# Logits of the last two batches from eight more output columns, and the placement of the last rows ahead of the border

## What is computed

```
x = x + attention(layernorm(x), ctx, ctx)    # 16 heads of 16; row i sees j < i (row 0 sees itself)
                                             # W_q, W_k, W_v, b_v, W_o, b_o
xt = layernorm(x) as 2048 rows
logits = xt @ wg                             # 8 experts
topv, topi = top_k(softmax(logits), 2); topv = topv / sum(topv)
pos = place of a row in its expert's queue: all first choices in row order, then all second choices
valid = pos < 512; gate = topv * valid; disp[topi, pos] += xt row where valid
h = relu(disp @ w1 + b1)                     # 256 -> 1024, for each expert
y = h @ w2 + b2                              # 1024 -> 256
out = x + sum over both choices of gate * y[topi, pos]
```

## Time and profile before

| | |
|---|---|
| median of three runs | 420.03 us (419.73 to 420.23) |
| the profiled execution | 422.05 us, of which the span is 420.3 |
| mean granted TensorE clock | 0.939 of full speed |
| busy: TensorE, its weight loads | 368.3 (88%), 315.2 (75%) |
| busy: VectorE, ScalarE, POOL | 294.4 (70%), 188.5 (45%), 214.6 (51%) |

### The profile page before, as it was taken

One profiled execution on the slowest core, in us unless ns is written; L12 is line 12 of the kernel. 1 busy time (PEld: TensorE's weight loads), 2 busy tenths in 40 slices (PEclk: granted clock), 3 DMA queues, 4 the chain that ended last, 5 costly groups with the idle time before them and its releaser, 6 DMA issues. The chain is left out here.

```text
span 420.3 us, 8189 instructions
## 1 busy us (share of the span) xinstructions
PE 368.3 (88%) x3030; PEld 315.2 (75%) x3030; DVE 294.4 (70%) x627; ACT 188.5 (45%) x258; POOL 214.6 (51%) x305
## 2 busy tenths in 40 slices
PE   3788889999999999777417999999999999999991
PEld 3656677878797877555305998989999999989891
DVE  6676778788887777837733777676778777776840
ACT  5423557565656557660203536263524435262410
POOL 8659866767677545250447008163463617060632
PEclk9988999999999999995556999999999999999998
DMA  7873815261706082413218009164363809040323
GB/s 219 236 215 121 212 31 153 76 193 39 201 14 191 18 218 83 153 51 114 52 38 292 22 2 264 51 218 97 134 176 75 240 18 272 27 58 2 37 27 37
DMA packets 38315, 49.15 MB, mean 117 GB/s; under 512 B 7138, under 2 KB 34180, under 8 KB 37252
## 3 DMA queue, kind: packets, MB, share of 16 engines
q1 hardware_dynamic: 29636, 34.93, 28.0%
q0 software_dynamic: 6144, 8.33, 10.5%
q10 hardware_dynamic: 2496, 5.38, 4.0%
HBM read 27.60 MB, written 8.41 MB: 86 GB/s over the span
## 5 line engine op out<-in xcount | busy, mean ns | idle before, releaser
L1578 POOL DMA_INDIRECT out_dram<-Y,scatter_idx x32 | 51.3, 1603 | 104.8 <-DVE Y L1734 89.4
L1621 ACT ACTIVATE hr<-ps,b_sb 128x512 f32<-128x512 f32 x64 | 43.2, 687 | 99.1 <-PE ps L1778 63.2
L764 DVE TENSOR_REDUCE nm<-ps 128x2 f32<-128x512 f32 (+1 forms) x96 | 62.5, 682 | 16.7 <-PE ps L1064 15.9
L1788 PE MATMUL ps<-w_hi,h_hi 128*128 128x256 f32 x224 | 63.2, 282 | 0.0
L1788 PE MATMUL ps<-w_lo,h_hi 128*128 128x256 f32 x224 | 62.5, 279 | 0.0
L1788 PE MATMUL ps<-w_hi,h_lo 128*128 128x256 f32 x224 | 62.5, 279 | 0.0
L529 ACT ACTIVATE PT<-ps 128x1536 f32<-128x1536 f32 x32 | 46.5, 1453 | 22.3 <-PE ps L1080 21.7
L1709 DVE CAST h_hi<-hr 128x512 fp32r<-128x512 f32 x60 | 27.5, 459 | 39.0 <-ACT hr L1621 38.9
L1778 PE MATMUL ps<-XT_hi,w_hi 128*128 128x512 f32 x128 | 51.5, 402 | 1.5 <-DVE XT_lo L1692 1.5
L1778 PE MATMUL ps<-XT_lo,w_hi 128*128 128x512 f32 x128 | 51.1, 399 | 0.0
L1778 PE MATMUL ps<-XT_hi,w_lo 128*128 128x512 f32 x128 | 51.1, 399 | 0.0
(11 more groups left out here) (234 smaller groups left out, 893.1 us busy)
## 6 DMA issues: line engine op xcount, KB each, us to landing
raw<-in_L_ffn_w_dram SPq DMA_DIRECT2D x12, 1024.0 KB, 8.2
raw<-in_L_ffn_w_dram ACTq DMA_DIRECT2D x4, 1024.0 KB, 5.5
c_sb<-in_ctx_dram SPq DMA_DIRECT2D x8, 256.0 KB, 3.8
xn_rows<-x2n SPq DMA_DIRECT2D x8, 256.0 KB, 3.0
out_dram<-x_all SPq DMA_DIRECT2D x8, 256.0 KB, 2.9
x_all<-in_x_dram SPq DMA_DIRECT2D x1, 1280.0 KB, 6.4
w_lo<-k_h SPq DMA_DIRECT2D x9, 128.0 KB, 2.5
w_hi<-q_h SPq DMA_DIRECT2D x9, 128.0 KB, 2.5
```

What stands on the lines that cost most here:

```text
L764: dve.tensor_reduce(nm[:, tile, h:h + count], max_bank[u % 2].rearrange("p (h j) -> p h j", h=count), AX_X, ALU.max, negate=True).then_inc ...
L1578: pool.indirect_dma_start(out_rows[:, :], bass.IndirectOffsetOnAxis(ap=scatter_idx[:, ST * e + j:ST * e + j + 1], axis=0), Y[q][:, j, :], ...
L1621: act.activation(hr[c % 2][:, :], h_bank[c % 4], ACT.Relu, bias=b1_sb[q][:, c:c + 1]).then_inc(hr_ready, 1)
L1788: last = pe.matmul(y_bank[j // 2][:, (j % 2) * D:(j % 2 + 1) * D], a[c % 4][:, j * P:(j + 1) * P], w[q][:, c, :], start=(c == 0 and n == 0 ...
```

## The change

1. **Logits without the turned x2n, for batches 6 and 7.** The layernorm's rows are (x - mean) times a factor, and the logit's order doesn't depend on the factor. x is the residual with its bias plus attention times W_o. So the kernel centres the router by its mean over the 256 inputs (wg_mid), puts W_o times wg_mid beside W_o as eight more columns (wo_hi and wo_lo have 264 columns), and gets eight logit columns from the same products that make the output rows (folded_outputs). The part from x with the bias is computed ahead: turn_biased, copy_biased, pre_router and copy_pre in step 7. sum_logits adds the two. The factor goes into the exponential (folded_ratio). turn_x2, copy_x2 and router fall away for these two batches; they stay for batches 0 to 5.
2. **What prepares this**, ahead of step 0: four transposes of W_o, the router's mean, and W_o times wg_mid, on TensorE between the score units of step -1, with copies on ScalarE and three small steps on VectorE.
3. **Early placement.** Its one-hot, counts, positions and numbers move from step 8 to step 7. The in_slot comparisons become 28 tensor_scalar of 128 elements with a scalar for each partition, where they were four tensor_tensor of 896; spart is f32 for this.
4. **Late placement, ahead of the border.** One-hot, counts, eq, in_slot (four tensor_scalar), late gates, table and gather_idx stand at the end of step 8. SP stores the late gates and then the last batch's output, and waits for all of it before the border. Behind the border POOL begins with the gathers.
5. **Weights of the first expert.** Parts 2 and 3 move from step 7 to step 8 on ScalarE, and behind the border on VectorE.
6. In step 7 POOL's mask of the last head group stands ahead of the powers of the layernorm, and on TensorE the transposes of x2n and the router give their places at the end of step 7 to early_counts and pre_router.

The core of the diff:

```diff
-    spart = sb("spart", [P, TOPK, EARLY], BF16)
+    spart = sb("spart", [P, TOPK, EARLY], F32)
...
+                if s == B:
+                    sp.wait_ge(gates_ready, 2)
+                    sp.dma_start(gate_tiles[:, 0:EARLY, :], gates[:, 0:EARLY, :]).then_inc(gates_stored, 16)
+                    for t in range(2):
+                        sp.wait_ge(x2n_ready, 2 * (s - 1) + t + 1)
+                        sp.dma_start(xn_tiles[s - 1][:, t, 0:D], x2n[:, t, :]).then_inc(x2n_stored, 16)
+                    sp.wait_ge(late_gates_ready, 2)
+                    sp.dma_start(gate_tiles[:, EARLY:, :], gates[:, EARLY:, :]).then_inc(gates_stored, 16)
+                    sp.dma_start(out_tiles[s - 1], x_all[:, 2 * (s - 1):2 * s, :]).then_inc(x2_stored, 16)
...
-            sp.wait_ge(gates_ready, 2)
-            sp.dma_start(gate_tiles[:, 0:EARLY, :], gates[:, 0:EARLY, :]).then_inc(gates_stored, 16)
-            sp.wait_ge(gates_stored, 16)
+            sp.wait_ge(gates_stored, 32)
             sp.wait_ge(spare_row, 32)
-            sp.wait_ge(x2n_stored, 16 * (B + 1))
+            sp.wait_ge(x2n_stored, 16 * (B + 2))
             sp.wait_ge(x2_stored, 16 * B)
...
                     mask(s, 2)
-                if out_part(s):
-                    powers(s - 1, ln2_stats, mv2, ve2, rs2, ln2_pow)
+                    mask(s, 3)
                 if s == B:
                     early_tiles(0)
                     early_tiles(1)
+                    last_powers(0)
+                    last_powers(1)
+                    late_gate()
+                    late_tiles()
+                elif out_part(s):
+                    powers(s - 1, ln2_stats, mv2, ve2, rs2, ln2_pow)
...
-                    first_weights(2, 3)
+                    copy_biased(0)
+                    copy_biased(1)
                     exp(s, 0)
                     round_attention(s)
                     exp(s, 1)
-                    first_weights(3, 4)
+                    copy_pre(0)
                     exp(s, 2)
                     values(s, 0)
                     exp(s, 3)
+                    copy_pre(1)
+                    values(s, 1)
                     normalise_x2(s)
-                    copy_x2(s)
-                    values(s, 1)
+                    early_ratio()
                     prefetch(3)
+                elif s == B:
+                    round_attention(s)
+                    early_rows()
+                    first_weights(2, 4)
+                    normalise_last(0)
+                    late_ratio()
+                    normalise_last(1)
+                    late_rows()
...
+            def sum_logits(s, t):
+                if t == 0:
+                    dve.wait_ge(pre_ready, folded(s) + 1)
+                dve.wait_ge(last_out, 2 * folded(s) + t + 1)
+                last = dve.tensor_tensor(lg[:, t, :], bank[t][:, D:D + EXPERTS], pre[:, folded(s), t], ALU.add)
+                if t == 1:
+                    last.then_inc(lg_ready, 1)
...
+            def last_rows():
+                n = B - 1
+                sum_logits(B, 1)
+                dve.wait_ge(lg_ready, n + 1)
+                for t in range(2):
+                    dve.max(top8[:, t, :], lg[:, t, :]).then_inc(top_ready, 1)
+                add_row_tile(B, 1)
+                dve.wait_ge(top_ready, 4 * n + 2)
+                for t in range(2):
+                    dve.max_index(idx8[:, t, :], top8[:, t, :], lg[:, t, :]).then_inc(top_ready, 1)
+                row_stats(B, 1)
+                dve.wait_ge(top_ready, 4 * n + 4)
+                for k in range(TOPK):
+                    dve.tensor_copy(expert_all[:, k, bass.ds(2 * n, 2)], idx8[:, :, k]).then_inc(top_used, 1)
+                dve.tensor_tensor(dl_all[:, bass.ds(2 * n, 2)], top8[:, :, 1], top8[:, :, 0], ALU.subtract).then_inc(top_used, 1)
+                row_moments(B, 1)
+                dve.wait_ge(top_used, 3 * n + 2)
+                late_onehots()
...
+            def late_places():
...
+                for k in range(TOPK):
+                    for t in range(2):
+                        last = dve.tensor_scalar(in_slot[:, k, EARLY + t, :], iota_s[:, :], late_spart[:, k, t:t + 1], None, ALU.is_equal)
+                last.then_inc(late_in_slot_ready, 1)
...
             def early_slots(k, n):
-                cols = slice(n * EARLY // 2, (n + 1) * EARLY // 2)
-                dve.tensor_tensor(in_slot[:, k, cols, :], spart[:, k, cols].unsqueeze(2).broadcast_to([P, EARLY // 2, P]),
-                                  iota_s[:, :].unsqueeze(1).broadcast_to([P, EARLY // 2, P]), ALU.is_equal).then_inc(in_slot_ready, 1)
+                for t in range(n * EARLY // 2, (n + 1) * EARLY // 2):
+                    last = dve.tensor_scalar(in_slot[:, k, t, :], iota_s[:, :], spart[:, k, t:t + 1], None, ALU.is_equal)
+                last.then_inc(in_slot_ready, 1)
...
-                    first_weights(2)
-                    add_output(s)
-                    dve.wait_ge(mask_done, 2 * GROUPS * (s + 1))
-                    first_weights(3)
-                    logits(s)
+                    add_rows(s, 0)
+                    sum_logits(s, 0)
+                    sum_logits(s, 1)
+                    top_two(s - 1)
+                    early_onehot()
+                    add_rows(s, 1)
+                    early_positions()
+                    early_numbers()
                 elif s == B:
-                    early_onehot()
                     normalise(s, 0)
                     normalise(s, 1)
-                    early_positions()
+                    early_groups()
+                    early_slots(0, 0)
                     split_attention(s)
-                    early_numbers()
-                    add_last(0)
-                    add_last(1)
-                    early_gates()
-                    early_groups()
-                    dve.wait_ge(ln2_pow, 4 * B)
-                    early_slots(0, 0)
                     early_slots(0, 1)
                     early_slots(1, 0)
                     early_slots(1, 1)
-                    logits(s)
+                    early_gates()
+                    add_rows(s, 0)
+                    sum_logits(s, 0)
+                    last_rows()
+                    late_places()
+                    late_gate()
+                    gather_rows()
...
+            def turn_output_weights():
+                pe.wait_ge(wqkvo_loaded[3], 16)
+                pe.wait_ge(k_rest_ready, 1)
+                pe.wait_ge(const_ready, 1)
+                turn(first_bank[1], lambda t: w_raw[:, 3, t, :], wo_turned)
...
+            def logit_weights():
+                pe.wait_ge(wg_mid_ready, 1)
+                pe.wait_ge(wo_copied, 1)
+                for f in range(2):
+                    for k in range(2):
+                        last = pe.matmul(first_bank[2][:, (2 + f) * EXPERTS:(3 + f) * EXPERTS], x2T[:, k, f * P:(f + 1) * P], wg_mid[:, k, :],
+                                         start=(k == 0), stop=(k == 1))
+                last.then_inc(wog_done, 1)
...
+            def pre_router(n):
+                pe.wait_ge(xb_copied, n + 1)
+                if n == 1:
+                    pe.wait_ge(pre_ready, 1)
+                for t in range(2):
+                    for k in range(2):
+                        last = pe.matmul(ps[:, 1, (2 * n + t) * EXPERTS:(2 * n + t + 1) * EXPERTS], xbT[n][:, k, t * P:(t + 1) * P],
+                                         wg_mid[:, k, :], start=(k == 0), stop=(k == 1))
+                last.then_inc(pre_done, 1)
...
+            def folded_outputs(s):
+                pe.wait_ge(aT_lo_ready, s)
+                pe.wait_ge(norm_done, 2 * s)
+                for t in range(2):
+                    m = 0
+                    for k in range(2):
+                        for a, w in ((aT_hi, wo_hi), (aT_lo, wo_hi), (aT_hi, wo_lo)):
+                            m += 1
+                            last = pe.matmul(fold_out(t), a[:, k, t * P:(t + 1) * P], w[:, k, :], start=(m == 1), stop=(m == 6))
...
-                    early_counts()
                     turn_last(lambda t: attn[:, t].rearrange("p h d -> p (h d)"), norm_done, at_done)
-                    last_outputs()
-                    turn_last(lambda t: x2n[:, t, :], x2n_ready, x2t_done)
+                    folded_outputs(s)
+                    late_counts()
                     early_table(0, 0)
-                    router(s)
                     early_table(0, 1)
                     early_table(1, 0)
                     early_table(1, 1)
+                    late_table()
...
+                    turn_biased(0)
+                    turn_biased(1)
                     turn_values(s, 0)
                     turn_values(s, 1)
                     b_scores(s, 0)
+                    pre_router(0)
                     turn_attention(s)
                     b_scores(s, 1)
                     values(s, 0)
                     b_scores(s, 2)
-                    outputs(s)
```

(18 more changed lines are left out.)

291 lines of the change are left out of this document (197 added, 94 removed).

## The result

The changed kernel takes 415.55 us (median of 14 runs, 414.24 to 420.76), the kernel before 420.62 (median of 14 runs, 419.71 to 428.36). The ratio is 0.9863, with a 95% interval of 0.9823 to 0.9902: 4 to 7 us less. Disturbed runs are left out of all ratios here. The forecast was 414.7 with a range of 411.2 to 418.6, faster. The profiled execution has a span of 414.4 us, against 420.3.

What follows compares the result with a forecast made beforehand. TensorE alone bounds from 224.38 us; VectorE's work ahead sets when the first gather starts. That gather 5.85 us sooner, less 0.5 ahead of attention, gives 5.3: 420.03 - 5.3 = 414.7 us, range 411.2 to 418.6.

Steps and rivals of the forecast that it cites:

- End of step 7: TensorE's first turn of step 8 starts at about 187.85 us, where it was 189.62.
- The clock: First turn of step 8 runs at 2.4 GHz, half of 1.95 us; normalisations end at 189.7, before 193.39.
- Comparisons and POOL: VectorE, eq to last sums: 28 comparisons 3.9 us, POOL's products 1.9, attention split 0.7, early gates 0.5.
- The dear rival: VectorE's small comparisons start 0.26 us apart: 28 cost 3.4 us more, the late four 0.5; 418.6 us; chance 0.14.
- the slower one: VectorE's small comparisons don't overlap, 0.35 us each: 32 cost 6.7 us more, 421.4 us; chance 0.07.
- The last logits: End of step 8, VectorE: 1.1 + 1.3 + 1.0 + 0.4 us bring the one-hot to 201.6, where it was 210.16.
- Late placement: End of step 8: one-hot to in_slot's end 2.8 us, gates ready at 205.0, VectorE done at 206.75.
- The border: Ahead of the gathers: the last output lands at 208.1, 1.35 us later than VectorE; border's 0.54 makes it 208.65.
- From the gather to layer 1: First gather to first layer-1 matmul: 8.95 us, carried over as unchanged.
- Ahead of attention: Added TensorE and VectorE work between the first score units costs 0.5 us, bounds 0 and 2.6.
- less in the way: Comparisons slip past POOL's products (-1.9), output lands before VectorE is done (-1.35), or both: 412.8, 413.3, 411.4; chance 0.22.
- The low clock at 188: TensorE at step 8's start is granted 1.2 GHz all the same, +0.9 us; chance 0.06, shared with the prologue case.

Runs made afterwards that it cites:

- e_chain: Changed kernel with the last batch's logits waiting again for the normalised, turned and routed x2n (results unused), both tiles' sums ahead; 423.74 us, 1.0046 of the kernel before.
- e_store: Changed kernel with the last batch's output stored as soon as its sums are there, ahead of x2n and the late gates; 415.27 us, 0.9863 of the kernel before.
- e_split: Changed kernel with the second half of the first expert's weight split on VectorE behind the turned rows; 416.57 us, 0.9892 of the kernel before.
- e_gate: Changed kernel with the output stored early and VectorE's late gates ahead of the late eq; 414.44 us, 0.9774 of the kernel before.
- e_best: e_order plus TensorE matmuls of no use, six in step 7 and 26 between border and layer 1; 411.0 us, 0.9733 of the kernel before.
- e_order: Changed kernel with large early comparisons, POOL's products behind them, early output store, late gates ahead of eq, later weight split; 415.14 us, 0.981 of the kernel before.

## Why the prediction was right, step by step

The forecast was 5.3 us; the medians are 5.07 apart, and the interval is 4 to 7. The total was right partly by luck: errors of both signs met, and they are listed below. In the columns above, forecast and measured (changed kernel less before, the first pair):

```
                    last softmax  to norms' end  to first gather  to layer 1  to the end
forecast                 +0.5         -3.7           -2.1            0            0
measured, first pair     -0.8         -2.9           -3.8           +0.9         +0.7
```

- **End of step 7.** Right. I had the first turn 4.74 us behind the start of the last softmax; it came 4.68 behind.
- **The clock.** Failed in this execution. I took the turn at 2.4 GHz; it ran at 1.2, and the normalisations ended 0.61 us later than with the fast turn. My reason was that early_counts and pre_router fill the gap; they stood there, and the clock fell all the same. It was named as a rival, with 0.9.
- **Comparisons and POOL.** From eq's end to the last sums I had 7.0 us; it was 7.11. The sum fits because its terms cancel: the 28 comparisons cost 4.6 instead of 3.9 (0.166 each against 0.14), POOL 1.5 instead of 1.9 (1.48 to 1.54), the split of attention 0.6 instead of 0.7. The dear rival (0.26) and the slower one (0.31 and more) are excluded by 21 in 3.49 us.
- **The last logits.** Mis-sized: 3.8 forecast, 2.83 measured (197.81 to 200.64). I added 1.0 for the second tile's three steps; they stand between steps of the logits that have to wait for one another, and filled gaps that I had counted as work. e_chain shows it: with the three steps ahead, it is 1.42 us there from the first sum of the logits to the end of the one-hot (209.62 to 211.04), and 1.81 here with them in between (198.83 to 200.64). So they cost 0.4, not 1.0.
- **Late placement.** Right: 3.4 us from the one-hot to the gates, measured 3.36 (200.64 to 204.00).
- **The border.** Right in kind: the output's landing is last, VectorE waits 1.63, and e_store brings that down to 0.55. Its size was 0.5 less: it landed in 2.2 us, not 2.7.
- **From the gather to layer 1.** Failed. The sentence "nothing of that is changed, so I carry it as it is" overlooked the weight split that the change puts there. I asked only whether the split fits beside the gathers in time, and not what it does to POOL meanwhile, although I had charged the same engines 1.9 us for each other one step earlier. It cost 0.73 (e_split).
- **Ahead of attention.** I took 0.5. One pair at nearly equal clock gives 0.25; the last softmax of eleven changed executions starts between 181.28 and 187.04, so the whole of it stays open within some us. From the first softmax to the last it is 143.6 to 145.3 us in the twelve changed executions, and 142.7 and 144.7 in the two of before, so a later begin of steps 1 to 6 by more than 1 us is not seen, and not excluded either.
- **Layer 1 to the end.** The 0.7 of the first pair is not the change's: the other executions without filling lie at 195.45 to 196.57, around before's 195.92.

The rivals: of "less in the way" neither half came true. The output landed earlier than forecast, but still 1.06 us behind VectorE (206.64 against 205.58), and the comparisons did not slip past POOL. The low clock at 188 came true in this execution, at 0.61 instead of 0.9.

Two smaller readings were wrong. VectorE was not "nearly without a gap" from 192 to 213 us before: it stood still for 1.31 us ahead of in_slot, waiting for POOL's powers of the layernorm (the row of before under e_chain). And a measurement can tell less than I took it to: I wrote 0.2%, and the interval of the ratio is 0.4% to either side.

## What to carry to other kernels

Before a step is moved off the critical engine, ask what it was the cover of: here, by the rows of before, taking one chain away would have given nothing as long as other work hid it (read from the trace, not run); with that work moved ahead it was worth 7 us. A block of work that is put "beside" another engine's must be priced twice, for its own time and for what it does to that engine. When a stretch of waiting stands ahead of a long run of matmuls, read the granted clock of the run's first microseconds: 26 matmuls of no use gave back more there (1.5 to 2.7 us, in two executions) than any single edit of order tried here (1.1 at most).

## What was not expected of the hardware

- Beside VectorE's two tensor_tensor on 1024 float32 POOL's first indirect gather took 1.96 us; without them it took 1.23. POOL's two products held VectorE's small bf16 comparisons too: seven took 2.70 us beside them, 1.22 alone. The products themselves took 1.84 in both cases.
- Small comparisons let POOL through (1.84 us for two products), four large ones don't (3.47), and the large ones are still the shorter way for VectorE, by 1.1 us beside the products and 0.56 without them.
- The granted clock of one place differs from execution to execution of the same code: the first turn of step 8 took 1.09 us in four executions of ten, 1.97 in five.
- The same store of the late gates landed 1.5 and 1.6 us after its issue in e_store and the changed kernel, where it was issued 1.1 us behind x2n's second tile, and 2.1, 2.2 and 2.7 us in e_gate, e_best and e_order, where it was issued 0.4 us behind it. No run separates the two.
